# Half-empty quarters of the attention probabilities are added and turned once; q's cosine product stays in PSUM

## The reference, cut to what matters

```python
h = shift_token(x)                        # second half of the channels comes from the row before
q, k, v = split(h @ wqkv)                 # 8 heads of 64
q, k = l2norm(q) * qs, l2norm(k) * ksc
q, k = rotary_xpos(q, k)                  # q * cos + rotate_half(q) * sin
# windows of 128 rows; each sees its own keys and those of the window before
mask = (i < j) | (i > j + WINDOW) | (j == -1)
attn = softmax(where(mask, -max, q @ k.T * 8))
x = x + (attn @ v) @ wo
h = layernorm(shift_token(x)) * lg + lb
a, g = split(h @ w1 + b1)
x = x + (a * gelu(g)) @ w2 + b2
```

## Time and profile before

| | us |
|---|---|
| median of 3 runs | 2688.95 |
| lowest, highest | 2684.12, 2690.76 |
| span of the profiled execution | 2682.5 |
| TensorE busy | 2626.4 |
| VectorE busy | 2276.5 |
| ScalarE busy | 1934.8 |
| GpSimd busy | 1658.1 |

### The profile page before, as it was taken

One profiled execution on the slowest core, in us unless ns is written; L12 is line 12 of the kernel. 1 busy time (PEld: TensorE's weight loads), 2 busy tenths in 40 slices (PEclk: granted clock), 3 DMA queues, 4 the chain that ended last, 5 costly groups with the idle time before them and its releaser, 6 DMA issues.

```text
span 2682.5 us, 65519 instructions
## 1 busy us (share of the span) xinstructions
PE 2626.4 (98%) x22240; PEld 2309.2 (86%) x22240; DVE 2276.5 (85%) x6866; ACT 1934.8 (72%) x4826; POOL 1658.1 (62%) x1753
## 2 busy tenths in 40 slices
PE   8999999999999999999999999999999999999998
PEld 5677688899998899998999898989988999988887
DVE  5778988888888888888888889898989989998786
ACT  5655588777777777777777777777777777778775
POOL 6523755566566556666665676666766667766563
PEclk9999999999999999999999999999999999999999
DMA  9931300000001100000001211011101111111110
GB/s 314 334 105 59 107 21 24 29 24 29 27 27 55 44 25 29 25 29 24 28 25 60 93 31 36 30 37 33 37 30 34 33 33 37 31 36 34 30 32 23
DMA packets 144510, 140.37 MB, mean 52 GB/s; under 512 B 16024, under 2 KB 126128, under 8 KB 143408
## 3 DMA queue, kind: packets, MB, share of 16 engines
q1 hardware_dynamic: 144176, 136.18, 16.0%
HBM read 80.02 MB, written 51.92 MB: 49 GB/s over the span
## 4 chain that ended last, share of the span: by engine, by line
PE 61%; DVE 2%; ACT 1%; issue 1%; DMA 1%; SPq 0%; POOL 0%; DVEq 0%; ACTq 0%; POOLq 0%
PE p_pair L173 13%; PE p_pair L174 10%; PE p_pair L175 10%; PE p_values L2551 6%; PE p_turn L2540 5%; PE p_mixed L173 4%; PE p_mixed L175 4%; PE p_mixed L174 4%; PE p_turn L2522 2%; PE p_turn L2516 1%; PE p_mixed L2486 1%; PE p_mixed L2568 1%; PE p_mixed L2594 0%; PE p_mixed L2593 0%; ACT prob L1224 0%
## 5 line engine op out<-in xcount | busy, mean ns | idle before, releaser
L960 POOL TENSOR_TENSOR prob<-prob,rinv 128x512 f32<-128x512 f32 (+1 forms) x512 | 506.5, 1001 | 393.0 <-DVE rinv L1771 392.7
L1224 ACT ACTIVATE prob<-prob,least 128x256 f32<-128x256 f32 (+1 forms) x1024 | 496.2, 487 | 63.2 <-DVE least L1763 61.7
L938 POOL TENSOR_TENSOR inv_norm<-norm_clipped,minus_half 128x8 f32<-128x8 f32 x256 | 423.0, 1659 | 79.2 <-DVE norm_clipped L1727 71.8
L1763 DVE CUSTOM_DVE_ANT_0 prob<-p_pair,mask,inv_norm 128x256 f32<-128x256 f32 (+1 forms) x1024 | 440.2, 460 | 35.0 <-PE p_pair L175 33.0
L173 PE MATMUL p_pair<-hT_h,w_h 128*128 128x256 f32 (+1 forms) x1408 | 410.1, 291 | 6.9 <-ACT v L1218 2.5
L174 PE MATMUL p_pair<-hT_l,w_h 128*128 128x256 f32 (+1 forms) x1408 | 391.1, 278 | 0.0
L175 PE MATMUL p_pair<-hT_h,w_l 128*128 128x256 f32 (+1 forms) x1408 | 391.0, 278 | 0.0
L1236 ACT ACTIVATE pT<-p_turn 128x512 f32<-128x512 f32 (+1 forms) x512 | 283.7, 569 | 76.3 <-PE p_turn L2540 63.9
L173 PEld LDWEIGHTS p_pair<-hT_h,w_h 128*128 128x128 f32 (+1 forms) x1408 | 262.6, 186 | 22.7 <-issue 10.8
L1835 DVE SCALAR_TENSOR_TENSOR gated<-p_pair,columns,gelu 128x256 f32<-128x256 f32 (+1 forms) x384 | 184.0, 481 | 108.5 <-ACT gelu L1263 106.4
L2540 PE MATMUL p_turn<-ident,prob 128*128 128x128 f32 x1920 | 266.5, 273 | 0.8 <-POOL prob L960 0.5
(11 more groups left out here) (147 smaller groups left out, 7970.3 us busy)
## 6 DMA issues: line engine op xcount, KB each, us to landing
x_tile<-x_rows SPq DMA_DIRECT2D x192, 128.0 KB, 2.1
a_wraw<-in_w_all SPq DMA_DIRECT2D x32, 264.0 KB, 5.3
w_high<-a_wraw_h SPq DMA_DIRECT2D x32, 264.0 KB, 3.9
w_low<-a_wraw_l SPq DMA_DIRECT2D x32, 264.0 KB, 4.7
a_x<-in_x SPq DMA_DIRECT2D x32, 256.0 KB, 4.2
x_rows<-a_x SPq DMA_DIRECT2D x64, 128.0 KB, 1.8
x_tile<-x_rows SPq DMA_DIRECT2D x128, 64.0 KB, 2.0
mid_rows<-x_mid SPq DMA_DIRECT2D x128, 64.0 KB, 1.7
```

The lines of the kernel that those rows point to most:

```text
L938: pool.tensor_tensor(r[:, t.slot(2), heads], rt[:, heads], half[:, heads], ALU.pow).then_inc(pool_r[n], 1)
L960: pool.tensor_tensor(p, p, rinv[:, 2 * m:2 * m + 2].unsqueeze(2).to_broadcast([P, 2, cols.stop - cols.start]), ALU.mult).then_inc(pool_p, 1)
L1224: act.activation(prob[:, h, cols], prob[:, h, cols], ACT.Exp, bias=least[:, h:h + 1], scale=-1.0, accum_out=rsum[:, h:h + 1]).then_inc(act ...
L1763: dve.tensor_tensor_reduce(prob[:, h, cols], p_score[h % 2][:, c0 + cols.start:c0 + cols.stop], mask[:, a.slot(2), cols], r[:, a.slot(2), ...
```

## The change

- A window's two half-empty off-diagonal quarters are brought together. GpSimd adds the quarter of the previous window's first 64 keys and that of the own window's last 64 keys (`mixed`, 128 x 8 heads x 64), and multiplies the sum by one over the sum of its row (normalise_mixed). The two other, full quarters of a head ("straight": own first and previous last 64 keys) are multiplied by it and written side by side into the middle 128 columns of its probabilities. normalise, turn_probs and probs_out work on 4 heads instead of 2, for straight quarters; turn_mixed turns two heads of the sum in one transpose, and mixed_out (ScalarE) places its live quarters in pT_mixed with four copies; the other corners of pT_mixed are zeroed once (zero_corners).
- v is laid out to match: v_out makes two copies of 64 partitions each, so that a slot holds the own first half and the previous last half, and copy_v (SP) builds the other combination v_mixed, a ring of 3, with two DMAs of 64 rows. values multiplies with both and waits for the DMAs, and for all three copies of turned probabilities.
- q's cosine product is written back into its PSUM bank (q_cos, after q_sin), and q_sum adds it from there; k's stay in SBUF. widen and project_q then wait for q_sum.
- x_mid and its shifted half lie in one tile, so that statistics and normed take one instruction each.
- rinv is doubled. Layer 1's v weights have no place of their own any more; they are loaded over layer 0's at the boundary (refill_v).
- x_new in layer 1 waits for an older `final`.
- All orders (first_on_*, step, last_steps) are drawn anew; the steady steps begin at 11 or 12, before at 8 to 11. In ScalarE's step the gelus are followed by exponential(T(4), 5 to 7); before, by probs_out(T(4), 0) and exponential(T(4), 4 to 7).

```diff
+    def straight(t):
+        own = t.slot(2)
+        if t.first:
+            return prob[:, :, own * P:own * P + P].rearrange("p h (c d) -> p h c d", d=D)
+        halves = prob[:].rearrange("p h (c d) -> p h c d", d=D)
+        return halves[:, :, 1:3] if own else halves[:, :, 0:4:3]
...
+        def copy_v(t):
+            n, own = t.slot(3), t.slot(4)
+            sp.wait_ge(act_v, t.done(1, 1))
+            need(sp, pe_pv, t.done(4, -8))
+            sp.dma_start(v_mixed[0:D, n], v[half_rows(source, source.slot(2)), source.slot(4)]).then_inc(v_mixed_in[n], 16)
+            sp.dma_start(v_mixed[D:P, n], v[half_rows(t, t.slot(2)), after.slot(4)]).then_inc(v_mixed_in[n], 16)
...
-        def normalise(a, m):
-                pool.tensor_tensor(p, p, rinv[:, 2 * m:2 * m + 2].unsqueeze(2).to_broadcast([P, 2, cols.stop - cols.start]),
-                                   ALU.mult).then_inc(pool_p, 1)
+        def normalise(a, group):
+                    own = a.slot(2) * P
+                    pool.tensor_tensor(mixed[:, heads], prob[:, heads, P - own:P - own + D], prob[:, heads, own + D:own + P],
+                                       ALU.add).then_inc(pool_mix, 1)
+                    if own == 0:
+                        pool.wait_ge(pool_mix, 2 * a.mixed() + group + 1)
+                    by_sum(a, heads).then_inc(pool_p, 1)
+        def normalise_mixed(a):
+                    pool.tensor_tensor(mixed[:], mixed[:], inverse.to_broadcast([P, H, D]), ALU.mult).then_inc(pool_p, 1)
...
-                act.activation(v[:, t.slot(4)], p_wide[0][:], ACT.Copy).then_inc(act_v, 1)
+                rows = half_rows(t, t.slot(2))
+                act.activation(v[rows, t.slot(4)], p_wide[0][0:D], ACT.Copy)
+                act.activation(v[rows, t.back(-1).slot(4)], p_wide[0][D:P], ACT.Copy).then_inc(act_v, 1)
...
+        def mixed_out(a):
+                for side in range(2):
+                    for half_ in range(2):
+                        rows = slice(half_ * D, half_ * D + D)
+                        ins = act.activation(pT_mixed[rows, side::2, rows],
+                                             p_turn[1][side * D:side * D + D].rearrange("p (m t) -> p m t", t=P)[:, :, rows],
+                                             ACT.Copy)
...
+        def q_cos(t):
+                q = p_wide[1][:].rearrange("p (h d) -> p h d", h=H)
+                dve.wait_ge(dve_qs, t.done(1, 1))
+                dve.tensor_tensor(q, q, tab[:, t.window, 0].unsqueeze(1).to_broadcast([P, H, D]), ALU.mult).then_inc(dve_qr, 1)
...
-                dve.bn_stats(st[:, n, 0], mid[:, n, 0:P])
-                dve.bn_stats(st[:, n, 1], shifted[:, n])
+                dve.bn_stats(st[:, n], shifted_h(n))
...
+        def turn_mixed(a):
+                for m in range(2 if a.first else H // 2):
+                    source = to_turn(a)[:, H - 2 + m] if a.first else mixed[:, 2 * m:2 * m + 2]
+                    ins = pe.transpose(p_turn[1][:, m * P:(m + 1) * P], source, ident[:])
...
         def values(a, m):
+                if m == 0:
+                    pe.wait_ge(v_mixed_in[a.slot(3)], 32 * a.uses(3, 1))
+                parts = [(mixed_v, pT)] if a.first else [(v[:, a.slot(4)], pT), (mixed_v, pT_mixed)]
```

More of the change, by code:

```diff
@@ L1759, in least_of @@
                         dve.wait_ge(pool_r[0], a.done(1, 1))
-                    need(dve, pe_pT, a.done(4, 2 * group - 2))
+                    need(dve, pe_pT, a.done(3, group - 2 + (group if a.g and a.back(1).first else 0)))
                 c0 = h % 4 // 2 * 2 * P
@@ L6059, in first_on_tensor @@
+    t.after((signal.dve_q, T(2), 1, 1))
+    t.turn_q(T(2))
+    t.values(T(0), 2)
     t.values(T(0), 3)
```

6304 lines of the change are left out of this document (3272 added, 3032 removed).

## The result

| | before | after |
|---|---|---|
| median of 4 runs each, us | 2686.53 | 2607.72 |
| lowest, highest | 2683.65, 2690.76 | 2602.12, 2611.52 |
| span of the profiled execution | 2682.5 | 2605.8 |

The ratio is 0.9702 (95% interval 0.9686 to 0.9719), 3.0% faster: 79 us, where 50 were forecast. The direction was right, and a gain of about 30 us was missed. The prediction's own extreme was 2601 us; it had drawn its lower bound in to 2615 by judgement, and the measured time lies between the two.

A forecast was written before the change was run, and what follows sets the result against it. TensorE, busy 98% of the span, was taken to bound the kernel. Span 2682.5 - 48.8 (transposes) - 7 (switches) + 6 (lateness) = 2632.7 us, 2639 us as a median, 1.9% faster; range 2615 to 2675 us.

The forecast's parts named there:

- What bounds the kernel, and counts: TensorE, busy 98% of the span, bounds the kernel; probability transposes fall from 1920 to 1472, a steady step to 36.2-36.4 us.
- nobody waits long for v's copies: Values' new wait for v's DMA copy: covered by over 30 us, so no cost.
- Fewer transposes, 0.109 us each, 48.8 us: TensorE: 448 probability transposes fewer, each priced by distance between starts at 0.109 us, 48.8 us saved.
- Rival 1: Tight chains around scores and turn_mixed give back half: 0.5 us late on 56 steps, 2661 us; chance 0.20.
- Switches -7, lateness +6: TensorE's steady steps: fewer changes between kinds of work save 7 us; lateness in two tight chains costs 6 us.
- the slack: Step's end, from the reciprocal through GpSimd's add and multiplies to turn_mixed: 0.27 to 0.57 us to spare.
- ScalarE and GpSimd hidden: Added copies, adds and multiplies: ScalarE +93 us to 77%, GpSimd +73 to 106 us to 66% busy, hidden as sums.
- VectorE -68 us, off the path: VectorE's q_sum and normalising get 0.53 us a window shorter, 68 us in all, without changing the forecast time.
- 231 ns of q_sum: VectorE's q_sum falls from 915 to 684 ns with the cosine product in PSUM.
- widen waits for q_sum, nothing is late: Widen waits for q_sum instead of the sine product; q_sum ends as scores(T(4), 1) runs, so no cost.
- Ends: "I take 0, bounds -12 and +15": Redrawn orders of the first and last windows, with some 50 us of idle time: no change, bounds -12 and +15 us.

The follow-up runs named there:

- turned_again: After with each of the four transposes of the summed quarters issued twice, 448 more in the new order: 2654.8 us, ratio to before 0.9891.
- sum_twice: After with GpSimd's add of the two quarters of heads 4 to 7 done twice, with a wait on itself: 2637.4 us, ratio to before 0.9823.
- vector_as_before: After with q's cosine product in SBUF again and normalising in two instructions: 2608.7 us, ratio to before 0.9724.

## Why the prediction was wrong, step by step

- *What bounds the kernel, and counts*: right. TensorE is at 98%, 1472 transposes, a steady step of 1587.8/44 = 36.09 us (forecast 36.2 to 36.4; the one step that the forecast started from took 37.15, the average of the steady part 36.86), and nobody waits long for v's copies: values waits 1.7 us in all for ScalarE and never for their DMAs, 2.3 us from issue to landing.
- *Fewer transposes, 0.109 us each, 48.8 us*: right in the new order, 47 to 49 us. But it was argued from before's order ("an instruction taken from TensorE is worth its full distance ... as long as no other chain takes over"), and there one does: 22 us. Rival 1's mechanism, chains that give back half, is what the old order does; the new one avoids it. The number is right with an incomplete reason, so luck has a part in it.
- *Switches -7, lateness +6*: together -1; turned_again, with before's number of matmuls, is 2.2 us faster in the steady part. Right as a sum; the two terms were not measured apart. sum_twice agrees with the size of the slack.
- *ScalarE and GpSimd hidden*: in the steady part the sum leaves little room for a cost of what was added (turned_again 1619.5, before 1621.7), but there was little to spare, and no run takes the additions away.
- *VectorE -68 us, off the path*: its busy time fell by 76 us, and the two parts that were undone give 0 and 3 us; the rest was not tried. The working was wrong: 231 ns of q_sum were taken from a mean that one view further would have shown to be a median of 686 with a tail. What the 915 ns bear out is a collision in 59 of 128 cases, not a price of each.
- *widen waits for q_sum, nothing is late*: true as it stands, but only with a margin. With 1 us a window more on VectorE this wait costs 16.4 us of the steady part.
- *Ends: "I take 0, bounds -12 and +15"*: this is the step that failed. They gave about 30 us: 11.7 at the start, 7.5 in the fill, 11.2 at the end by the profiles of before and turned_again, 29 in the medians (2654.8 against 2684.0). At the start it is mainly the order of the first attention (6 to 8 us). In the fill and the end the runs show, in place of the 0, fewer changes of kind (46 and 42 fewer, 0.15 us for one among the values), and at the end waits at the transposes as well. The prediction had this price in its hands: it counted one or two switches fewer in each of the 56 full steps and none in the ends, where the new orders have 88 fewer. It sought the ends' time in TensorE's idle time, some 50 us. Of the 32.8 us between the spans of these two kernels, which have the same matmuls, only 7.9 were idle time in before (56.1 against 48.2); 24.9 were counted as busy (2626.4 against 2601.5). The granted clock explains little: over the first 289 us it is 0.96 in both, and the time at its lower level is 27.3 against 20.5 us up to the first output and 8.1 against 4.7 at the end, at most 3.4 and 1.7 us. The distances between starts would have shown it: up to window 12's output in before 368 value matmuls take 26.2 us, 0.071 each, where in a steady step 32 take 1.90, 0.059.

The sum with the measured terms: 2686.5 - 48 (transposes) - 30 (start, fill and end) - 2 = 2607.

## What to carry to other kernels

Where an order is drawn anew by hand or planner, count how often the bounding engine changes its kind of work in the ends of both orders, and price the ends from the distances between starts against those of the steady part, not from idle time. A saving on the bounding engine is worth its distance only if the order lets the next chain keep up; the same 448 transposes gave 22 us in one order and 48 in the other. Before a price is taken from a mean, look at its minimum, median and maximum.

## What the runs showed of the hardware

- A 512-column matmul that is followed by a 128-column transpose hides a wait of 0.14 us in its records: 1.61 us from start to start in place of 1.46 to 1.48, and TensorE's record shows no idle time there.
- A break in the value matmuls costs 0.15 us with no wait: 8 of them take 0.59 us to the next kind, 32 take 1.90.
- VectorE's add of 128x512 with two SBUF inputs takes 686 ns as a median and up to 1660; with one input in PSUM 676 to 694. 53 of the 59 long ones began beside GpSimd's k_sum. Writing the product into the PSUM bank that is being read costs next to nothing (692 ns; into SBUF 688 for k's and 683 for q's in vector_as_before).
- Copies of 64 partitions cost ScalarE what 128 cost (585 and 594 ns for 512 columns; 594 for 128 partitions).
- Up to the first output, profiles of kernels with the same attention order differ by 6 to 10 us, with the granted clock at its lower level for 10 to 38 us; behind it the two profiles of after differ by 2 us or less a stretch.
